# Final transposes and stores moved into the expert stage, three gathers for groups past the end left out

## The reference, cut to what matters

```
t = t + _L1_ffn_ref(_ln_t(t), gate_w, w1, b1, w2, b2)    # B=4 images, 1024 tokens each, 256 channels
x = _from_tokens(t, x)                                   # (b, token, channel) -> (b, channel, token)

for e in range(E):                                       # E = 8, hidden size 1024
    h = gelu(x_flat @ w1[e].T + b1[e])
    y = h @ w2[e].T + b2[e]
    out = out + comb[:, e:e + 1] * y                     # comb: softmax weights of the two chosen experts
```

## Time and profile before

| what | value |
|---|---|
| time, median of 3 executions | 1497.94 us (1493.28 to 1498.65) |
| the profiled execution: its own time | 1492.93 us |
| the profiled execution: its span | 1491.0 us |
| busy share of PE, DVE, ACT, POOL | 82%, 54%, 46%, 37% |
| mean granted TensorE clock | 0.91 |
| DMA traffic from HBM and to HBM | 66.71 MB read, 60.96 MB written |

### The profile page before, as it was taken

One profiled execution on the slowest core, in us unless ns is written; L12 is line 12 of the kernel. 1 busy time (PEld: TensorE's weight loads), 2 busy tenths in 40 slices (PEclk: granted clock), 3 DMA queues, 4 the chain that ended last, 5 costly groups with the idle time before them and its releaser, 6 DMA issues. The chain is left out here.

```text
span 1491.0 us, 27981 instructions
## 1 busy us (share of the span) xinstructions
PE 1220.6 (82%) x9389; PEld 827.7 (56%) x9390; DVE 798.9 (54%) x1573; ACT 692.0 (46%) x1318; POOL 559.0 (37%) x475
## 2 busy tenths in 40 slices
PE   3979998933997798879887985744999999999983
PEld 1546665621334434533443343633888888888872
DVE  3855655445465656466655343873544545545441
ACT  3565544436577566756775741421323233332311
POOL 3977554111900370043000000025355555555652
PEclk9999999966999999899998997555999999999996
DMA  5756889824970794099209503873444444444437
GB/s 169 171 140 142 182 178 195 166 77 71 242 197 1 138 272 128 1 162 248 72 7 197 165 1 121 325 243 106 60 66 79 74 82 68 81 72 78 74 62 239
DMA packets 331506, 192.01 MB, mean 129 GB/s; under 512 B 273824, under 2 KB 311968, under 8 KB 329248
## 3 DMA queue, kind: packets, MB, share of 16 engines
q1 hardware_dynamic: 296928, 130.48, 37.4%
q0 software_dynamic: 26144, 59.34, 17.3%
q10 hardware_dynamic: 8352, 1.08, 0.5%
HBM read 66.71 MB, written 60.96 MB: 86 GB/s over the span
## 5 line engine op out<-in xcount | busy, mean ns | idle before, releaser
L2043 ACT ACTIVATE moe_shared<-moe_hbank,moe_b1T 128x256 f32<-128x256 f32 x312 | 130.7, 471 | 270.3 <-PE moe_hbank L1975 266.6
L1975 PE MATMUL moe_hbank<-moe_rowT,l_w1T 128*128 128x256 f16 x1872 | 213.5, 275 | 13.1 <-DMA moe_rowT<-moe_ends 12.9
L1990 PE MATMUL moe_ybank<-l_w2T,moe_shared 128*128 x1872 | 210.6, 273 | 0.0
L1975 PEld LDWEIGHTS moe_hbank<-moe_rowT,l_w1T 128*128 x1872 | 184.1, 99 | 37.1 <-issue 14.6
L1990 PEld LDWEIGHTS moe_ybank<-l_w2T,moe_shared 128*128 128x128 f16 x1872 | 183.2, 98 | 21.2
L1170 ACT ACTIVATE block_probs<-block_bank 128x1024 f32<-128x1024 f32 (+1 forms) x192 | 144.3, 808 | 74.2 <-PE block_bank L932 61.8
L801 POOL COPY block_stack<-block_stack 128x512 f16<-128x512 f16 x16 | 10.6, 664 | 362.2 <-ACT block_stack L1154 362.2
L1907 POOL DMA_INDIRECT acc_scratch<-moe_ends,moe_which x78 | 129.8, 1664 | 42.3 <-issue 23.7
L2224 DVE TENSOR_SCALAR moe_shared<-moe_shared 128x2048 f16<-128x2048 f32 x39 | 49.0, 1257 | 169.3 <-ACT moe_shared L2043 169.3
L929 PE MATMUL block_bank<-block_qkT 128*128 128x512 f16 (+3 forms) x384 | 94.6, 334 | 47.7 <-issue 24.3
L300 POOL TENSOR_SCALAR front_raw<-front_raw 128x1024 f32<-128x1024 f32 x32 | 92.0, 2874 | 53.6 <-ACT conv_probs L525 53.2
(11 more groups left out here) (348 smaller groups left out, 2448.0 us busy)
## 6 DMA issues: line engine op xcount, KB each, us to landing
front_raw<-in_L_ffn_w POOLq DMA_DIRECT2D x32, 512.0 KB, 5.3
w_turned<-block_qk SPq DMA_DIRECT2D x32, 512.0 KB, 3.6
w_parts<-front_raw_hi POOLq DMA_DIRECT2D x32, 256.0 KB, 5.6
w_parts<-front_raw_lo POOLq DMA_DIRECT2D x32, 256.0 KB, 6.3
l_w1T<-w_turned SPq DMA_DIRECT2D x8, 1024.0 KB, 11.1
l_w2T<-w_turned SPq DMA_DIRECT2D x8, 1024.0 KB, 12.0
rows_scratch<-moe_ends SPq DMA_DIRECT2D x4, 1056.0 KB, 5.4
front_shared<-in_x SPq DMA_DIRECT2D x8, 512.0 KB, 6.9
```

Of the source, the lines that this page charges most:

```text
L1975: last = pe.matmul(hbank[:, c, :], w1T[:, e, wp, k, c * P:(c + 1) * P], rowT[q][:, xp * CC + k, :], start=n == 0, stop=n == 5)
L1990: last = pe.matmul(ybank[q][:, t, :], (hid_hi, hid_lo)[hp][q][:, c, t * P:(t + 1) * P], w2T[:, e, wp, c, :], start=n == 0, stop=n == 3 * H ...
L2043: act.activation(hid[:, c, :], hbank[:, c, :], ACT.Gelu, bias=b1T[:, e, c:c + 1], scale=1.0 / (GAIN * GAIN)).then_inc(S["gelu_done"], 1)
```

## The change

The block `write_out` is gone. Its work stands at the end of each engine's list in the block of the experts, so that there is one barrier less. Its loads wait on SP for `added` and go into `sums`, its results into `images`: both are views of the SBUF memory of `w1T`, the first weights of the experts (one half each), and both hold all 4 images, so that no copy waits for a store. Eight PSUM banks of the expert stage (`out_bank`) take the place of four. The stores are issued by SP, behind the loads on the same queue, and no longer by POOL. For POOL the last loop round is written out (`all_tiles(pool, step, 1)`: 8 rounds and 4 steps), and a step whose group j + 3 does not exist issues no gather. The steps of the other engines are as before.

```diff
-        def all_tiles(eng, step):
+        def all_tiles(eng, step, apart=0):
             for j in range(3):
                 step(j, j)
-            with eng.Fori(0, (GROUPS - 3) // 4) as i:
+            with eng.Fori(0, (GROUPS - 3) // 4 - apart) as i:
                 for r in range(4):
                     step(i * 4 + (3 + r), (3 + r) % 4)
+            for j in range(GROUPS - 4 * apart, GROUPS):
+                step(j, j % 4)
+
+        def image_copies(eng, copy, sem, parity):
+            for b in range(B):
+                for n in range(parity, 2 * CC, 2):
+                    eng.wait_ge(S["image_full"], b * 2 * CC + n + 1)
+                    copy(images[:, b, n // 2, n % 2 * 512:(n % 2 + 1) * 512], out_bank[b % 2 * 4 + n]).then_inc(sem, 1)
...
                 all_tiles(sp, step)
+                sp.wait_ge(S["added"], GROUPS * 16 * GT)
+                src = acc[0:B * T, :].rearrange("(b t p) d -> b p t d", p=P, t=T // P)
+                for b in range(B):
+                    for h in range(2):
+                        ts = slice(h * T // P // 2, (h + 1) * T // P // 2)
+                        sp.dma_start(sums[:, b, ts, :], src[b][:, ts, :]).then_inc(S[f"sums_loaded{2 * b + h}"], 16)
+                for b in range(B):
+                    for c in range(CC):
+                        sp.wait_ge(S["image_copied"], b * CC + c + 1)
+                        sp.wait_ge(S["image_copied_act"], b * CC + c + 1)
+                        sp.dma_start(out[b, c * P:(c + 1) * P].rearrange("p h w -> p (h w)"), images[:, b, c, :]).then_inc(S["image_stored"], 16)
+                sp.wait_ge(S["image_stored"], 16 * CC * B)
...
-                    gather(j + AHEAD, (r + AHEAD) % 4)
+                    if not isinstance(j, int) or j + AHEAD < GROUPS:
+                        gather(j + AHEAD, (r + AHEAD) % 4)
...
-                all_tiles(pool, step)
+                all_tiles(pool, step, 1)
...
                 down(GROUPS - 1, (GROUPS - 1) % 4)
+                for b in range(B):
+                    for n in range(2 * CC):
+                        c, h = n // 2, n % 2
+                        pe.wait_ge(S[f"sums_loaded{2 * b + h}"], 16)
+                        if b >= 2:
+                            pe.wait_ge((S["image_copied"], S["image_copied_act"])[n % 2], (b - 2) * CC + n // 2 + 1)
+                        for i in range(4):
+                            last = pe.transpose(out_bank[b % 2 * 4 + n][:, i * P:(i + 1) * P], sums[:, b, h * 4 + i, c * P:(c + 1) * P], ident[:, :])
+                        last.then_inc(S["image_full"], 1)
...
-        write_out(nc, acc, out, ident)
```

More of the change, by code:

```diff
@@ L1700, with route_and_experts @@
 TURNS = 4
-def route_and_experts(nc, acc, rows, ident, gate_w, w1_turned, w2_turned, b1, b2, w1T, w2T, w_loaded, expert_of):
+def route_and_experts(nc, acc, rows, ident, gate_w, w1_turned, w2_turned, b1, b2, w1T, w2T, w_loaded, expert_of, out):
     PER = TILES // TURNS
@@ L1769, in route_and_experts @@
         xbank = [s.ps(f"xbank{i}", [P, 512]) for i in range(2)]
+        sums, images = (w1T[:, i * (E_N // 2):(i + 1) * (E_N // 2), :, :, :].rearrange("p e a k h -> p (e a k h)").bitcast(F32) for i in range(2))
+        sums = sums.rearrange("p (b t d) -> p b t d", b=B, t=T // P)
+        images = images.rearrange("p (b c t) -> p b c t", b=B, c=CC)
+        out_bank = [hbank[:, 2 * n:2 * n + 2, :].rearrange("p c q -> p (c q)") for n in range(4)]
+        out_bank += [x[:, :] for x in xbank] + [x[:, :, :].rearrange("p t d -> p (t d)") for x in ybank]
         lbank, pbank = (hbank[:, c, 0:PER * E_N].rearrange("p (t e) -> p t e", e=E_N) for c in (6, 4))
@@ L1776, in route_and_experts @@
                  "lane_hot", "col_hot", "col_valued", "spread", "slots_known", "which_set", "weighed",
-                 "bias_loaded", "h_full", "gelu_done", "hi_done", "lo_done", "y_full", "ysum_done", "y_done", "added", "passed")
+                 "bias_loaded", "h_full", "gelu_done", "hi_done", "lo_done", "y_full", "ysum_done", "y_done", "added", "passed",
+                 *(f"sums_loaded{i}" for i in range(2 * B)), "image_full", "image_copied", "image_copied_act", "image_stored")
         S = {n: s.sem(n) for n in names}
@@ L1908, in step @@
                                                 y[r % 2][:, t, :], None, compute_op=ALU.add).then_inc(S["added"], 16)
-                all_tiles(pool, step)
+                all_tiles(pool, step, 1)
                 pool.wait_ge(S["added"], GROUPS * 16 * GT)
                 for r in range(4):
-                    pool.wait_ge(S[f"got{r}"], 32 * len(range(r, GROUPS + AHEAD, 4)))
+                    pool.wait_ge(S[f"got{r}"], 32 * len(range(r, GROUPS, 4)))
             @block.tensor
@@ L2046, in _ @@
                 all_tiles(act, step)
+                image_copies(act, lambda o, i: act.activation(o, i, ACT.Copy), S["image_copied_act"], 1)
             @block.vector
@@ L2251, in _ @@
                 dve.wait_ge(S["y_done"], GROUPS)
[L2254 to L2313, removed]
@@ L2316, in build @@
+                image_copies(dve, dve.tensor_copy, S["image_copied"], 0)
 def build(nc, x, p, out):
@@ L2383, in build @@
             route_and_experts(nc, acc, rows, ident, p["L1_ffn_gate_w"], w1_turned, w2_turned, p["L1_ffn_b1"], p["L1_ffn_b2"],
-                              w1T, w2T, w_loaded, expert_of)
-        write_out(nc, acc, out, ident)
+                              w1T, w2T, w_loaded, expert_of, out)
 _INS = ["x"] + [f"L0_conv_{n}" for n in ("norm_gamma", "norm_beta", "wq", "bq", "wk", "bk", "wv", "bv", "wp", "bp")] \
```

## The result

The changed kernel took 1484.95 us in the median of 9 executions (1478.82 to 1490.01) against 1498.65 us for the kernel before (1491.88 to 1502.80); the ratio is 0.9907, with a 95% interval of 0.9888 to 0.9927. So it is faster, by the ratio by 13.9 us with 11 to 16.8 as the interval, where my steps added up to 8.6.

What follows compares the result with a forecast made beforehand. PE bounds the expert steps, untouched; behind them POOL's scatters, the barrier and DMA transfers set the end. First load 7.9 us earlier (3.9 gathers, 4.0 barrier) plus 0.7 in the last stage: -8.6 us, 1497.94 to 1489.3, range 1483 to 1494.5.

Steps and rivals of the forecast that it cites:

- three stretches behind PE's last matmul: POOL's scatters up to 1460.8, the block's end and barrier up to 1465.03, then 26.0 us of transfers; the change edits each.
- POOL's tail: POOL's scatters in the expert stage's last steps: without gathers the last one lands 3.9 us earlier.
- start-up of 0.84 us: POOL, steps 37 and 38: a scatter begins 0.84 us after the semaphore it waits for, as in step 0.
- rival without start-up: POOL prepares the scatter during the wait: 1.7 us more gain, -10.3 us, 1487.6; chance 0.12.
- release and start-up together: POOL, step 38: 0.27 us from the landing of step 37's scatter to release, then 0.83 us to the next scatter.
- The barrier: Between last scatter's landing and first load: 4.2 us shrink to SP's own wait of 0.2 us, 4.0 us gained.
- The last stage: Final loads and stores, DMA-bound: 25.3 us (1.4 + 12.0 + 10.2 + 1.7) against 26.0, 0.7 us less.
- a limit of 358 GB/s: Skill page's limit of a core's HBM traffic: 8.39 MB take 23.4 us, final stage 26.5 us, 0.5 us more.
- the rule which speaks against the change: Final stores on SP's queue wait for all loads by ring order, losing the mixed 414 GB/s; sum said unchanged.
- Slow stores behind the loads: Final stores on SP's queue run at 357 GB/s: -7.0 us in all, 1490.9; chance 0.17.
- Gathers not waited for: Gathers do not hold up POOL's scatters, so only the barrier goes: -4.7 us, 1493.2; chance 0.04.
- SP holding back its stores one by one: Each final store begins only when the one before landed, 3.6 us each: net +10.0 us, 1507.9; chance 0.02.

Runs made afterwards that it cites:

- joined alone: Changed kernel with POOL's loop and gathers as before, only the final block joined to the expert stage's; ratio to the kernel before 0.9971 (0.9949 to 0.9993).
- the run with POOL's stores: Changed kernel with its 8 stores issued by POOL on its own queue, not by SP; ratio to the kernel before 0.9963, last stage 32.1 us.

## Why the prediction was right, and where its sizes were off

*Where the time goes.* Right: the gain lies in three stretches behind PE's last matmul and nowhere else.

*POOL's tail.* Right in mechanism, 0.8 us too small. I had the second scatter of step 38 at 4.3 us behind DVE's end, it stood at 3.9 (mean of three), and the tail of before was 8.6 in the mean and not 8.2. The start-up of 0.84 us that I took from step 0 was 0.89 us in step 37 (1445.37 to 1446.26), so the rival without start-up is refuted, although its gain of 10.3 us is nearer to the measured one than mine. From a landing to the next scatter it was less than I had: 1448.12 + 3.7 = 1451.8 to 1452.59, 0.8 us and not the 1.1 of my release and start-up together.

*The barrier.* Right: 4.3 us against 4.0 (joined alone, and the changed kernel). SP issued at once with the landing and did not need the 0.2 us.

*The last stage.* The time of the changed kernel was right (25.3 forecast; 25.8, 25.1 and 25.0 measured; first 350, then 414 GB/s), but the gain was not: 1.6 us against 0.7. The term that was mis-sized is the 26.0 us for the stage before. It was one execution, and the quickest of three. The row of the loads' landings with its maximum of 12.5 us, which my sum did not use, says where it varies: in the four traces with that last stage the last load lands 12.5 to 14.3 us after its issue and the stage takes 26.0 to 28.2. The 26.5 us worked out from a limit of 358 GB/s did not come: the stores moved 414.

*The order on one queue.* I wrote that the rule which speaks against the change alters nothing in the sum. For the sum of the changed kernel that was true. But it hid what the order is for: without it the wider room gives 28.8 and 32.1 us against 25.3, of which 3 to 3.5 us are transfers that end later. The full DMA share that I took as proof that only bytes count says nothing about whose bytes they are.

*The rivals.* Slow stores behind the loads (357 GB/s): refuted by 414. Gathers not waited for: refuted. SP holding back its stores one by one: refuted; they landed 8.4 us (median) after their issue and moved 414 GB/s without a gap.

*The sum.* 8.6 us forecast, 10.5 us by six traces, 10.6 by the mean of three ratios. The missing 1.9 us are 0.8 in POOL's tail, 0.3 at the barrier and 0.9 in the last stage, rounded. The time was forecast as 1489.3 us and measured as 1484.95; of these 4.3 us some 3 belong to the first ratio and did not come back in two repetitions, which gave 1486.85 and 1486.92.

## What to carry to other kernels

When loads feed stores, ask which of them the queues let through first: a full set of DMA engines can be busy with stores while the last load starves, and the end then stands alone. Here it helped to put the stores behind the loads on the same queue, or to give both the same piece size; the wider buffers without one of the two made the stage longer. And where a stage's length is to be a term of a sum, take it from several traces, or read the spread of its landings.

## What was not expected of the hardware

The queues of SP and ACT shared the DMA engines by count of packets, not by bytes: 445 and 442 packets in 5 us gave 1.63 and 0.44 MB; 109 and 110 in 2 us gave 0.45 and 0.41 MB. SP's and POOL's did so over 6 us of the kernel before (541 and 525), but not in every stretch (368 and 239). In the run with POOL's stores 20 of the loads' last packets took 4 us, and 4.8 us without any visible work stood at the end. Loads alone moved 353 GB/s in pieces of 1 KB and 369 in pieces of 4 KB, where stores on the same queue moved 414.
